# A two-layer graph and expert block: layer A's normed rows on ScalarE and GpSimd, layer B's convolution read from PSUM, one gate product, layer B's rows turned batch by batch

## What is computed

```python
h = layernorm(x)                              # layer A, 12 heads of 32
q, k, v = h @ Wq.T, h @ Wk.T, h @ Wv.T + bv
p = softmax(q @ k.T * 384**-0.5 + 2 * adj)    # a row of scores that is all zero gives 0
x = x + (p @ v) @ Wo.T + bo
h = layernorm(x)                              # layer B, 3 experts of 128
gate = softmax(relu(h @ Wg1 + bg1) @ Wg2 + bg2); w = softmax over its best two
q, k, v = h @ Wqk + bqk, h @ Wv[e] + bv[e]
q[0] = conv(q[0], conv_w, 3 taps over the rows) + conv_b
y[e] = w[e] * (causal_softmax(q[e] @ k[e].T * 128**-0.5) @ v[e])
x = x + concat(y) @ Wp + bp
```

## Time and profile before

| | |
|---|---|
| median of 3 runs (lowest, highest) | 2337.28 us (2335.55, 2337.88) |
| profiled execution, its own time | 2333.05 us |
| its span, first to last instruction | 2331.3 us |
| mean granted TensorE clock, as a share of the full one | 0.974 |

### The profile page before, as it was taken

One profiled execution on the slowest core, in us unless ns is written; L12 is line 12 of the kernel. 1 busy time (PEld: TensorE's weight loads), 2 busy tenths in 40 slices (PEclk: granted clock), 3 DMA queues, 4 the chain that ended last, 5 costly groups with the idle time before them and its releaser, 6 DMA issues.

```text
span 2331.3 us, 53112 instructions
## 1 busy us (share of the span) xinstructions
PE 2044.0 (88%) x16557; PEld 1229.2 (53%) x16557; DVE 2092.0 (90%) x7150; ACT 1576.0 (68%) x5458; POOL 1739.9 (75%) x2065
## 2 busy tenths in 40 slices
PE   3689898889988899899898988998989898988878
PEld 1355555555555555555555555555555555555545
DVE  4899999999899999988999999999999999999985
ACT  2676666776666776666776666766666766666764
POOL 1787777777778777778777778777778777778773
PEclk9799999999999999999999999999999999999999
DMA  6645656555556555556555656555556565556531
GB/s 182 108 99 111 117 117 141 107 114 107 116 121 140 101 116 113 118 119 128 110 113 114 118 123 128 107 115 115 118 124 127 107 114 117 119 123 128 107 75 41
DMA packets 650185, 269.18 MB, mean 115 GB/s; under 512 B 524720, under 2 KB 649264, under 8 KB 649904
## 3 DMA queue, kind: packets, MB, share of 16 engines
q1 hardware_dynamic: 647712, 264.52, 54.7%
q10 hardware_dynamic: 2192, 1.29, 0.2%
HBM read 39.18 MB, written 25.17 MB: 28 GB/s over the span
## 4 chain that ended last, share of the span: by engine, by line
DVE 55%; PE 20%; POOL 12%; issue 10%; SPq 1%; DMA 1%; ACT 1%; DVEq 0%; POOLq 0%; ACTq 0%
DVE S L1008 12%; PE B_bank L550 8%; PE A_bank L550 7%; DVE smax L1014 6%; DVE h_parts L974 5%; DVE V L998 5%; POOL h L1185 3%; POOL rstd L1182 3%; DVE S L1022 3%; DVE b_hT_lo L974 2%; DVE q2raw L921 2%; DVE bn L855 2%; DVE q_lo L980 2%; DVE row2f L1047 1%; PE B_bank L630 1%
## 5 line engine op out<-in xcount | busy, mean ns | idle before, releaser
L765 ACT ACTIVATE S<-S,smin 128x128 f32<-128x128 f32 x1536 | 593.3, 388 | 47.9 <-DVE smax L1014 47.8
L1167 POOL TENSOR_TENSOR S<-S,rowf 128x512 f32<-128x512 f32 x384 | 399.3, 1069 | 143.6 <-DVE rowf L1039 143.6
L1141 POOL TENSOR_TENSOR P_parts<-S,P_parts 128x512 f16<-128x512 f32 x384 | 476.3, 1256 | 9.3 <-ACT P_parts L706 7.2
L1008 DVE CUSTOM_DVE_ANT_0 S<-A_bank,adj,s_unit 128x128 f32<-128x128 f32 x1536 | 431.9, 343 | 15.0 <-PE A_bank L618 14.6
L765 ACT ACTIVATION_READ_ACCUMULATOR S<-S,smin 128x1 f32 x1536 | 288.0, 188 | 0.0
L706 ACT ACTIVATE P_parts<-S 128x512 f16<-128x512 f32 x384 | 229.0, 619 | 43.0 <-POOL S L1167 42.8
L729 ACT ACTIVATE b_hT_hi<-B_bank 128x512 f16<-128x512 f32 x96 | 53.6, 596 | 260.0 <-PE B_bank L595 260.0
L1014 DVE TENSOR_REDUCE smax<-S 128x12 f32<-128x1536 f32 x128 | 223.1, 1743 | 0.1
L550 PE MATMUL A_bank<-wv_hi,h1T 128*128 128x384 f16 x768 | 204.7, 329 | 2.8 <-DVE wv_lo L798 2.8
L550 PE MATMUL A_bank<-h1T,wq_hi 128*128 128x512 f16 x576 | 174.6, 385 | 28.7 <-DMA h1T<-h_parts 28.7
L550 PE MATMUL A_bank<-h1T,wk_hi 128*128 128x512 f16 x576 | 173.5, 383 | 22.4 <-DVE oT_lo L987 22.4
(11 more groups left out here) (183 smaller groups left out, 6153.2 us busy)
## 6 DMA issues: line engine op xcount, KB each, us to landing
xin<-in_x SPq DMA_DIRECT2D x32, 768.0 KB, 4.6
Qs<-q_hi SPq DMA_DIRECT2D x256, 96.0 KB
out<-x1res SPq DMA_DIRECT2D x128, 192.0 KB, 2.1
Ks<-k_hi SPq DMA_DIRECT2D x252, 96.0 KB
Qs<-q_lo SPq DMA_DIRECT2D x128, 96.0 KB
Ks<-k_lo SPq DMA_DIRECT2D x126, 96.0 KB
adj<-in_adj SPq DMA_DIRECT2D x32, 256.0 KB, 2.8
PT<-P_parts SPq DMA_TRANSPOSE x384, 3.2
```

The lines of the kernel that those rows point to most:

```text
L765: ins = nc.scalar.activation(S[b % 2][:, h, :], S[b % 2][:, h, :], ACT.Exp, bias=smin[b % 2][:, h:h + 1], scale=-1.0, accum_out=ssum[b % 2 ...
L1008: ins = nc.vector.tensor_tensor_reduce(S[b % 2][:, h, :], src[:, j * T:(j + 1) * T], adj2[:, b, :], s_unit[:], 3.0e38, ALU.add, ALU.min, s ...
L1141: nc.gpsimd.tensor_tensor(P_parts[:, c, 1, :], S[b % 2][:, c * HPC:(c + 1) * HPC, :].rearrange("p j k -> p (j k)"), P_parts[:, c, 0, :], A ...
L1167: nc.gpsimd.tensor_tensor(S[b % 2][:, hs, :], S[b % 2][:, hs, :], rowf[b % 2][:, hs].unsqueeze(2).broadcast_to([P, HPC, T]), ALU.mult).the ...
```

## The change

- POOL makes `-mean * rstd` and a `rstd` that holds the factor 64; ACT's new step `A.h1` makes the normed rows from `xin` with these as bias and scale, POOL's new step `A.hT` the low part. SP's transpose waits for the latter.
- ACT no longer writes `q2raw`. `conv` reads the bank of B.qk.0; since that holds q without its bias, the middle tap's bias takes in all three taps, and two additions on the first and last row of each batch take the surplus off. The bank is free after `conv`.
- ACT's new step `B.hid` takes the Relu of the gate columns; DVE makes the three gate products in one instruction, from a gate weight row stored once for each batch.
- `B.hT` has four steps in place of three: one batch, all three column blocks. It waits for that batch's `h2` alone; `v` waits for its batch, `qk` for all.
- The stores have a semaphore for each batch. All lists are written anew (the repeated one stands here; the first and last ones are cut).

```diff
 ORDER_OF_STEPS = {
     "pe": """
-        A.score.0.0 A.score.0.1 A.score.0.2 A.v.0 A.score.1.0 A.score.1.1 B.hT.0 B.hT.1 B.hT.2 A.score.1.2 A.v.1
-        A.v.2 B.qk.0 B.qk.1 A.score.2.0 B.v.0 A.score.2.1 B.v.1 A.v.3 B.qk.2 A.score.2.2 B.qk.3 B.v.2 B.v.3
-        B.qk.4 B.qk.5 A.score.3.0 A.score.3.1 A.mix.0 A.score.3.2 A.qk.0 A.qk.1 A.qk.2 B.score.0 A.qk.3
-        B.score.1 A.mix.1 A.qk.4 A.proj.0 B.score.2 A.qk.5 B.turn.0 A.mix.2 B.score.3 B.turn.1 B.mix.0 A.proj.1
-        B.mix.1 B.proj.0 A.proj.2 B.turn.2 B.proj.1 B.turn.3 A.mix.3 B.mix.2 B.mix.3 A.proj.3 B.proj.2 B.proj.3
+        B.hT.0 B.hT.1 A.score.0.0 A.score.0.1 A.score.0.2 A.score.1.0 A.v.0 A.score.1.1 A.v.1 B.hT.2 B.hT.3
+        A.score.1.2 B.v.0 B.qk.0 B.qk.1 A.score.2.0 A.v.2 B.qk.2 A.score.2.1 A.v.3 B.v.1 A.score.2.2 B.v.2
+        A.score.3.0 A.score.3.1 A.score.3.2 B.v.3 B.qk.3 B.qk.4 B.qk.5 A.mix.0 A.qk.0 A.qk.1 A.qk.2 B.score.0
+        B.score.1 A.proj.0 A.qk.3 A.qk.4 A.mix.1 B.turn.0 B.score.2 A.qk.5 B.mix.0 A.mix.2 A.proj.1 B.score.3
+        B.turn.1 B.proj.0 B.mix.1 A.proj.2 B.proj.1 B.turn.2 B.turn.3 A.mix.3 B.mix.2 B.mix.3 A.proj.3 B.proj.2
+        B.proj.3
     """,
     "act": """
-        B.hT.0 A.v.0 B.hT.1 B.hT.2 A.score.0.0 A.score.0.1 A.score.0.2 B.qk.0 B.qk.1 A.hT.0 A.turn.0.0 A.hT.1
-        A.v.1 A.turn.0.1 A.score.1.0 A.turn.0.2 A.score.1.1 A.score.1.2 B.qk.2 A.hT.2 B.qk.3 A.hT.3 A.turn.1.0
-        A.score.2.0 A.score.2.1 A.turn.1.1 A.turn.1.2 A.score.2.2 A.v.2 A.v.3 A.mix.0 B.qk.4 A.qk.0 B.qk.5
-        A.turn.2.0 A.qk.1 A.turn.2.1 A.turn.2.2 A.qk.2 A.score.3.0 A.score.3.1 A.score.3.2 A.qk.3 B.gate.0
-        B.score.0 B.gate.1 A.mix.1 A.qk.4 B.score.1 A.turn.3.0 A.turn.3.1 B.turn.0 A.turn.3.2 B.score.2 A.mix.2
-        B.mix.0 B.turn.1 B.score.3 A.qk.5 B.mix.1 B.turn.2 B.turn.3 A.mix.3 B.mix.2 B.mix.3
+        B.hT.0 B.hT.1 A.v.0 B.hT.2 B.hT.3 A.score.0.0 A.score.0.1 A.score.0.2 B.qk.0 A.h1.0 A.h1.1 A.hT.0
+        A.turn.0.0 B.qk.1 A.turn.0.1 A.hT.1 A.turn.0.2 A.h1.2 B.qk.2 A.v.1 A.h1.3 A.score.1.0 A.score.1.1 A.hT.2
+        A.hT.3 A.score.1.2 A.score.2.0 A.turn.1.0 B.hid A.score.2.1 A.turn.1.1 A.turn.1.2 A.score.2.2 B.gate.0
+        B.qk.3 B.qk.4 A.qk.0 A.mix.0 A.turn.2.0 A.v.2 B.qk.5 A.turn.2.1 A.qk.1 A.v.3 A.turn.2.2 A.score.3.0
+        A.qk.2 B.gate.1 B.score.0 A.score.3.1 A.score.3.2 A.mix.1 B.score.1 A.qk.3 B.turn.0 A.turn.3.0 A.qk.4
+        A.qk.5 A.turn.3.1 A.turn.3.2 B.mix.0 B.score.2 B.turn.1 A.mix.2 B.score.3 B.mix.1 B.turn.2 B.turn.3
+        A.mix.3 B.mix.2 B.mix.3
     """,
     "dve": """
-        A.score.0.0 A.score.0.1 A.v.0 A.score.0.2 B.hT.0 A.smax.0 B.hT.1 B.hT.2 A.ln1 A.score.1.0 A.score.1.1
-        A.norm.0 A.score.1.2 A.v.1 A.smax.1 A.hT.0 B.v.0 A.hT.1 B.v.1 A.score.2.0 A.score.2.1 A.score.2.2
-        A.norm.1 A.smax.2 A.hT.2 A.hT.3 A.v.2 B.v.2 B.conv A.v.3 A.score.3.0 A.norm.2 B.v.3 A.score.3.1
-        A.score.3.2 A.qk.0 A.smax.3 A.qk.1 A.mix.0 A.qk.2 B.score.0 B.gate.0 A.norm.3 B.gate.1 B.score.1
-        B.gate.2 B.norm.0 A.qk.3 B.norm.1 B.score.2 A.mix.1 A.qk.4 B.score.3 A.proj.0 B.norm.2 B.mix.0 A.mix.2
-        A.qk.5 A.proj.1 B.norm.3 B.proj.0 B.mix.1 B.proj.1 A.ln2.0 A.mix.3 B.mix.2 A.proj.2 A.ln2.1 B.mix.3
-        A.proj.3 A.ln2.2 B.proj.2 A.ln2.3 B.proj.3
+        B.hT.0 B.hT.1 A.score.0.0 A.score.0.1 A.score.0.2 A.v.0 A.smax.0 B.hT.2 B.hT.3 A.ln1 A.score.1.0 A.v.1
+        A.norm.0 A.score.1.1 B.v.0 A.score.1.2 B.conv A.smax.1 A.v.2 A.score.2.0 A.score.2.1 A.score.2.2 B.v.1
+        A.smax.2 A.norm.1 B.v.2 B.v.3 A.v.3 B.gate.0 A.score.3.0 A.norm.2 A.score.3.1 A.score.3.2 A.qk.0 A.mix.0
+        A.smax.3 B.gate.1 B.score.0 A.qk.1 A.qk.2 B.gate.2 B.score.1 B.norm.0 A.proj.0 A.norm.3 B.norm.1 A.qk.3
+        A.mix.1 A.qk.4 A.qk.5 B.score.2 B.mix.0 B.score.3 A.ln2.0 A.mix.2 B.norm.2 A.proj.1 B.mix.1 B.proj.0
+        B.norm.3 B.proj.1 A.proj.2 A.mix.3 A.ln2.1 B.mix.2 A.ln2.2 A.proj.3 B.mix.3 A.ln2.3 B.proj.2 B.proj.3
     """,
     "pool": """
-        B.res.0 A.vl.0 A.ln1 A.h1.0 A.h1.1 A.norm.0 A.turn.0.0 A.turn.0.1 A.h1.2 A.turn.0.2 A.res.0 A.h1.3
-        A.norm.1 A.vl.1 A.turn.1.0 A.turn.1.1 A.turn.1.2 A.norm.2 A.turn.2.0 A.turn.2.1 B.res.1 A.turn.2.2
-        A.res.1 A.vl.2 A.res.2 A.norm.3 B.norm.0 B.norm.1 A.turn.3.0 A.adj A.turn.3.1 A.turn.3.2 B.norm.2
-        B.res.2 A.vl.3 B.res.3 B.norm.3 A.ln2.0 A.res.3 A.ln2.1 A.ln2.2 A.ln2.3
+        A.vl.0 B.res.0 B.res.1 A.res.0 A.ln1 A.norm.0 A.hT.0 A.hT.1 A.turn.0.0 A.turn.0.1 A.turn.0.2 A.res.1
+        A.hT.2 A.hT.3 A.vl.1 A.norm.1 A.turn.1.0 A.turn.1.1 A.turn.1.2 A.norm.2 A.turn.2.0 A.turn.2.1 A.turn.2.2
+        A.res.2 A.vl.2 A.res.3 B.res.2 B.norm.0 A.norm.3 A.turn.3.0 B.norm.1 A.turn.3.1 A.turn.3.2 A.vl.3
+        B.norm.2 B.norm.3 B.res.3 A.ln2.0 A.ln2.1 A.adj A.ln2.2 A.ln2.3
     """,
     "sp": """
-        A.hT.0 A.turn.0.0 A.hT.1 A.turn.0.1 A.turn.0.2 A.hT.2 A.hT.3 A.turn.1.0 A.turn.1.1 A.turn.1.2 A.adj
+        A.hT.0 A.hT.1 A.turn.0.0 A.turn.0.1 A.turn.0.2 A.hT.2 A.hT.3 A.turn.1.0 A.turn.1.1 A.turn.1.2 A.adj
         A.turn.2.0 A.turn.2.1 A.turn.2.2 A.stack.0 A.turn.3.0 A.turn.3.1 A.turn.3.2 A.stack.1 B.proj.0 B.proj.1
...
-    return None if step[:2] == ("A", "turn") else "dve" if step[:2] == ("A", "qk") else EVAC.get(step[1])
+    return None if crossed(step) else "dve" if step[:2] == ("A", "qk") else EVAC.get(step[1])
...
-        hT_hi, hT_lo = (sb(f"b_hT_{p}", [P, KC, GB * T], F16) for p in ("hi", "lo"))
+        hT_hi, hT_lo = (sb(f"b_hT_{p}", [P, GB, KC, T], F16) for p in ("hi", "lo"))
...
-                wait_evacuated(eng, *ring[step[0]][n])
+                held, of = ring[step[0]][n]
+                if held == ("B", "qk", 0, 0):
+                    eng.wait_ge(conv_step, count(of, 4, 4))
+                else:
+                    wait_evacuated(eng, held, of)
...
-                    wait_evacuated(sp, step, g)
+                    sp.wait_ge(h1_lo, count(g, GB, b + 1))
...
-                wait_hT = (lambda c: wait_evacuated(pe, ("B", "hT", c, 0), g)) if b == 0 and not A else None
+                if kind in ("qk", "v") and b == 0 and not A:
+                    wait_evacuated(pe, ("B", "hT", GB - 1 if kind == "qk" else 0, 0), g)
+                elif kind == "v" and not A:
+                    wait_evacuated(pe, ("B", "hT", b, 0), g)
...
-                    if b == 0:
-                        pe.wait_ge(h2_ready, count(g, GB, GB))
-                    for n in range(GB):
-                        mm = nc.tensor.transpose(dst[:, tok(n)], h2[:, n, b * P:(b + 1) * P], ident[:])
+                    pe.wait_ge(h2_ready, count(g, GB, b + 1))
+                    for n in range(KC):
+                        mm = nc.tensor.transpose(dst[:, tok(n)], h2[:, b, n * P:(n + 1) * P], ident[:])
...
-                    nc.scalar.activation(h1_parts[:, b % 2, 0, :], h1[:, b % 2, :], ACT.Copy, scale=H_SCALE)\
+                    nc.scalar.activation(h1_parts[:, b % 2, 0, :], h1[:, b % 2, :], ACT.Copy)\
                         .then_inc(hi_ready["ahead"], 1)
+                elif kind == "h1":
+
+                    act.wait_ge(rstd1_done, count(g, 1, 1))
+                    if b >= 2 or not g == 0:
+                        act.wait_ge(h1_lo, count(g, GB, b - 1))
+                    nc.scalar.activation(h1[:, b % 2, :], xin[g % 2][:, b, :], ACT.Identity,
+                                         bias=stat[g % 2][:, 0, b:b + 1],
+                                         scale=stat[g % 2][:, 1, b:b + 1]).then_inc(h1_ready, 1)
                 elif kind == "hT":
                     wait_products(act, step, g)
-                    nc.scalar.activation(hT_hi[:, b, :], src[:, :], ACT.Copy, scale=H_SCALE)\
+                    nc.scalar.activation(hT_hi[:, b, :, :].rearrange("p c t -> p (c t)"), src[:, 0:C], ACT.Copy,
+                                         scale=H_SCALE)\
...
-                        nc.scalar.activation(q2raw[:], src[:, :], ACT.Identity, bias=bqk_col[:, 0:1],
-                                             scale=hinv[:, 3:4])
...
+                elif kind == "hid":
+
+                    wait_evacuated(act, ("B", "v", GB - 1, 0), g)
+                    nc.scalar.activation(g_hid[:], V2[:, :, C:VG], ACT.Relu).then_inc(hid_ready, 1)
...
-                    dve.wait_ge(conv_step, count(g, 2, 2))
-                    for e in range(NE):
-                        ins = v.scalar_tensor_tensor(out=g_prod[:, e], in0=V2[:, :, C:VG], scalar=0.0,
-                                                     in1=wg2_row[:, e, :].unsqueeze(1).broadcast_to([P, GB, GH]),
-                                                     op0=ALU.max, op1=ALU.mult)
-                    link(ins)
-                    link(v.tensor_reduce(sel[:], g_prod, AXX, ALU.add))
+                    dve.wait_ge(hid_ready, count(g, 1, 1))
+                    link(v.tensor_tensor(g_prod[:].rearrange("p e b n -> p e (b n)"),
+                                         g_hid[:].rearrange("p b n -> p (b n)").unsqueeze(1).broadcast_to(
```

(53 more changed lines are left out.)

186 lines of the change are left out of this document (102 added, 84 removed).

## The result

The changed kernel takes 2275.9 us (median of 4 runs, 2273.8 to 2276.9) against 2336.7 (4 runs): ratio 0.9739, 95% interval 0.9722 to 0.9755. Forecast were 2182 us and a range of 2110 to 2255: the sign was right, but the gain was 61 us and not 155, and the time lies above the range. The profiled execution took 2273.78, its span is 2271.7, its mean granted clock 0.970.

What follows compares the result with a forecast made beforehand. DVE was taken to set the pace, PE 1.4 us behind; after the change PE binds at 65.3 us a turn for 70.2. 2333 - 147 - 8 = 2178, as a median 2182 us, range 2110 to 2255.

Steps and rivals of the forecast that it cites:

- The sum on DVE: DVE's busy time a turn: savings of 4.5 + 1.1 + 1.5 - 0.4 = 6.7 us take 64.8 to 58.1.
- The convolution: On DVE, read from PSUM: two products of 0.73 and two edge additions of 0.17, 1.8 for 2.89, saving 1.1 a group.
- The gate product: On DVE, one product over 384 columns at 0.957 us replaces three of 0.855, saving 1.5 (1.0 to 1.9).
- fourth rival: POOL's queue: POOL's idle time of 16.1 us doesn't shrink, 71.5 us a turn, 2376 us; chance 0.07.
- the ends: Start and end of the kernel: 8 us saved at the end, 0 at the start (bounds -2 and +3).
- rival 3: SP's stack of K: the chain from A.norm.3's row factor to the next score sets 67.2 us a turn, 2239; chance 0.10.
- The sum on PE: PE binds: 70.2 - 2.6 - 1.2 - 1.0 - 0.4 + 0.3 = 65.3 us a turn, 4.9 saved over 30 turns.
- layer B's normed softmax: PE's wait for POOL's normed rows, 1.7 us a turn: stays, shortened by 0.4 by B.norm.0 and gate.2 standing earlier.
- slow stretch: PE matmuls at the lower clock behind the wait for V2's copy: gone, 1.2 us a turn, down to 62.2.
- wait for `V2`: PE's wait for DVE's copy that frees a bank of ring B: all 2.6 us a turn go with DVE's lateness.
- bank of B.qk.0: Held until the convolution is done, B.v.1 on PE waits for it: 0.3 us a turn added (bounds 0 and 1.8).
- The second rival: The lock: port shared with POOL lengthens DVE's edge additions and gate product by 1.65, 66.95 a turn, 2231 us; chance 0.13.

Runs made afterwards that it cites:

- experiment 5: Steady instruction lists of the kernel before, with the new functions and the few steps they need put in: 2492.1 us, ratio to before 1.0667.
- experiment 9: Changed kernel with three POOL additions (A.res.2, A.res.3, B.res.2) moved out of the run ahead of B.norm.0: 2189.0 us, ratio to before 0.9377.
- experiment 1: Changed kernel with B.turn.0 moved behind B.score.2 and A.qk.5 in PE's list: 2207.0 us, ratio to before 0.9458.
- experiment 2: Changed kernel with the gate's two-operand DVE instructions made single-operand reductions, its arithmetic left out: 2159.3 us, ratio to before 0.9255.
- experiment 8: Changed kernel with batch 3's row maxima on DVE reading 8 columns of each head instead of 128: 2269.0 us, ratio to before 0.9716.
- experiment 10: Changed kernel with the two maxima of gate.2 as single-operand reductions over pairs in one buffer: 2209.3 us, ratio to before 0.9466.

## Why the prediction was off

**The sum on DVE** (58.1 forecast, 60.4 measured). Layer A's low part went as forecast: no `h_parts` group is left on DVE. The convolution takes 0.449 + 0.734 + 0.231 + 0.740 = 2.15, forecast 1.8: the two products right, the edges 0.68 instead of 0.34. The gate product takes 1.445, just above the longest of the range (1.427) and not its median 0.957. And the gate's nine small products, which the change doesn't touch, were not in the sum: 4.75 a turn against 3.05 before. Of the first edge addition the timeline shows the same thing as of the products (it starts with its engine free and ends at 1160.65, within 0.03 us of a POOL instruction). In the changed kernel the second one, 0.231, doesn't show it; in experiment 5 both do: they take 0.78 and 0.43 and end within 0.03 us of a POOL instruction, at 1121.50 and 1122.61. The Trainium skill, "SBUF — State Buffer", "Who interferes with whom", counts tensor_scalar among the operations that can take the shared pair of ports, in a two-port mode; the trace agrees. In the sums, the upper bound of the convolution (1.3) should be 1.4, and the fourth rival's 2376 leaves out the 8 of the ends; neither enters the forecast or its range.

**ACT and POOL.** They work 50.8 and 53.1 us a turn, where 51.4 and 55.4 were forecast, and as busy time both are off the path. The K stack (rival 3) and POOL's queue (rival 4) didn't decide: in the steady turns PE never waits for `Ks`, and DVE's scores never for the buffer that POOL frees. The fourth named an idle time of 15 on POOL as its sign, and 15.1 is measured, but the sign was a poor one: experiment 9 has the same list in all but three words and 65.3 a turn.

**The sum on PE: the step that failed.** It said that the wait for layer B's normed softmax "stays, shortened by B.norm.0 and gate.2 standing earlier (-0.4)", and that the slow stretch goes with the wait for `V2`. The wait grew from 1.7 to 2.3, and the slow matmuls moved behind it: the second half runs at a mean of 0.92, while in the kernel before it had 1.00. Of the 2.9 us a turn between 65.3 and 68.2, 1.0 is this wait (2.3 for 1.3), 1.3 is PE's busy time (63.5 for 62.2), and 0.6 the other waits (2.4 for 1.8). Among these the wait for `V2` failed too: the sum took all of its 2.6 off, and 1.5 stayed. Part of that is hidden, because the small waits that the sum kept came to 0.9 instead of 1.5, and the 0.3 for the bank of B.qk.0 didn't come. What holds `V2`'s copies up no run looks into. Two things on the page of the diff were passed over. In PE's list B.turn.0 had moved ahead of B.score.2 and A.qk.5, the work that covered its wait (experiment 1). And the gate, now in one stretch with POOL's run of norm 2 to B.res.2, hung on that run (experiments 2, 8, 9, 10). Undoing either one takes the larger part of the missing 94 us away: experiment 1 gives 69, experiment 9 87.

**The second rival** had the right mechanism with the wrong place and size: the shared port, priced as 1.65 us of DVE's busy time on the edges and the gate product, where 0.83 came. Its sign, edge additions with a median above 0.5, did not come (0.459 and 0.231). What decided was not the sum of the waits but where the last one ends: the path went from DVE's row factor over POOL's ten instructions to the gate's last product.

**The ends** gave nothing for the 8 forecast. The first load of `xin` starts 5.0 us later (123.0 for 118.0), where 0 was forecast with bounds of -2 and +3. From the last load to the end of the span pass 170.3 us instead of 176.8; the shorter last turn is 2.0 of this, so the end gave some 4.5 and the start took them back. What holds the start up no run looks into. The ends also account for the 7 us that experiment 9 still lacks.

**What was right**: the time that PE itself needs, 62.2 a turn at the upper clock (62.1 in experiment 9). That the turn of experiment 9 is 65.3, the forecast to the tenth, is luck: a wait for `V` of 1.5 that the forecast had at nothing stands in it, and the others come to 1.5 less than it had.

## What to carry to other kernels

A sum of busy times names the engine that binds over a whole turn; where two engines take turns as the bound, cut the turn where one hands over to the other and make the sum for each part, following the one chain that joins them. When lists are written anew, look at each waiting step for the work that used to stand ahead of it on its own engine: a step moved forward by two places can cost more than a saved instruction gives. Short DVE instructions with two SBUF operands that stand beside a gapless run of POOL end when one of its instructions does (0.84 to 0.91 us here for 0.15 and 0.16), so move the run, or do without the second operand, before cutting anything ahead of them.

## What the runs showed of the hardware

- A DVE product on 4 columns took 0.162 or 0.837, by where it stood beside POOL; ahead of the end of POOL's run 1.06 us of a cut of 1.5 us on DVE came back as longer products (experiment 8).
- Behind a wait of PE of 2.3 us a turn the second half ran at a mean clock of 0.92; with the waits of experiments 9 and 10 (0.7 and 1.4 a turn) the mean over the turns was 1.00. PE's busy time is 62.1 a turn in both (1760.0 and 1742.8 us in 1850, by turns of 65.3 and 65.9), against 63.5: by this difference, an estimate, the long wait costs some 1.4 us beside its own length.
